# One index copy for two groups of gathers in the first two edge passes of a graph network

## The reference, cut to what matters

```python
# layer 0: messages along the edges, then a GRU cell
src_h = h[src] @ W_msg.T + b_msg
msg = src_h + edge_embed[clip(edge_type_9)]
messages = segment_sum(msg, dst, num_segments=12500)
x = x + gru_cell(messages, h)
...
# layer 1: graph convolution
msg = (deg_inv_sqrt[row] * deg_inv_sqrt[col])[:, None] * h[row]
agg = segment_sum(msg, col, num_segments=12500)
x = x + layernorm(agg @ W.T + b) * gamma + beta
```

## Time and profile before

| | us |
|---|---|
| median of 3 runs | 10787.66 |
| lowest and highest of them | 10783.5, 10787.84 |
| the profiled execution, its own time | 10766.11 |
| span of its trace | 10764.3 |
| first pass: first copy of indices to last | 127.5 to 2441.3 |
| second pass: first copy of indices to last | 2491.0 to 4811.0 |

### The profile page before, as it was taken

How to read it: one execution, slowest core, us unless ns; L and a number is a source line. 1 busy time by engine, 2 the same in 40 slices (tenths; PEclk the granted TensorE clock), 3 DMA queues, 4 the chain that set the end, 5 groups by cost and what they waited for, 6 DMA issues and landing times. The chain is left out here.

```text
span 10764.3 us, 142924 instructions
## 1 busy us (share of the span) xinstructions
PE 7296.1 (68%) x34582; PEld 5598.5 (52%) x34582; DVE 4890.2 (45%) x12591; ACT 1824.8 (17%) x4365; POOL 7100.4 (66%) x7075
## 2 busy tenths in 40 slices
PE   2655556555566666668888888888836666666666
PEld 1444445443333333336777777777624555555555
DVE  5444444445566666663222222222264555555556
ACT  1111111111111111112222222222221111111111
POOL 3666666665666666666888888888816555555553
PEclk6555555555555555556777777777755555555555
DMA  6122221222222222224444444444472222222221
GB/s 237 57 58 57 59 59 57 59 59 60 77 73 76 75 75 77 76 71 64 55 55 55 55 55 55 55 55 55 52 214 68 68 67 69 67 66 68 65 68 50
DMA packets 809415, 765.67 MB, mean 71 GB/s; under 512 B 128472, under 2 KB 701362, under 8 KB 809073
## 3 DMA queue, kind: packets, MB, share of 16 engines
q0 software_dynamic: 375872, 414.65, 21.5%
q1 hardware_dynamic: 340391, 271.94, 8.2%
q10 hardware_dynamic: 92938, 77.03, 2.3%
HBM read 544.72 MB, written 224.78 MB: 71 GB/s over the span
## 5 line engine op out<-in xcount | busy, mean ns | idle before, releaser
L1408 POOL DMA_INDIRECT scat<-msg_out,msg_idx x1564 | 2432.7, 1555 | 491.8 <-issue 421.7
L1997 POOL DMA_INDIRECT soft_rows<-proj,soft_slot x1564 | 1488.0, 951 | 1360.6 <-DVE soft_x L2184 690.2
L723 POOL DMA_INDIRECT L_rows<-H,L_slot x1568 | 1502.0, 958 | 691.3 <-issue 652.4
L988 POOL DMA_INDIRECT L_rows<-H,L_slot x1568 | 1498.2, 955 | 684.5 <-issue 618.0
L1501 PE MATMUL msg_ps_msg<-msg_hb,msg_lhs 128*128 128x128 f32 x6272 | 1600.3, 437 | 1.2 <-DVE msg_lhs L1474 1.2
L1501 PEld LDWEIGHTS msg_ps_msg<-msg_hb,msg_lhs 128*128 128x128 f32 x6272 | 1493.0, 328 | 191.8 <-issue 190.3
L1474 DVE SCALAR_TENSOR_TENSOR msg_lhs<-msg_dst_sp,msg_node,msg_ps_c 128x512 f32<-128x512 f32 x784 | 551.1, 745 | 2056.4 <-ACT msg_dst_sp L1429 2032.6
L859 PE MATMUL L_sum<-L_onehot,L_rows 128*128 128x64 f32 x3136 | 699.8, 394 | 782.9 <-issue 693.5
L859 PEld LDWEIGHTS L_sum<-L_onehot,L_rows 128*128 128x128 f32 x3136 | 648.7, 303 | 865.7 <-issue 851.8
L2126 PE MATMUL soft_ps_sum<-soft_onehot,soft_x 128*128 128x64 f32 x3136 | 753.1, 422 | 317.2 <-DVE sums_b L2243 226.1
L2126 PEld LDWEIGHTS soft_ps_sum<-soft_onehot,soft_x 128*128 128x128 f32 x3136 | 705.5, 328 | 383.9 <-issue 283.7
(11 more groups left out here) (365 smaller groups left out, 10487.9 us busy)
## 6 DMA issues: line engine op xcount, KB each, us to landing
L_rows<-H,L_slot POOLq DMA_INDIRECT x3136
msg_hb<-HB SPq DMA_DIRECT2D x392, 128.0 KB
soft_at_in<-in_edge_attr_dram SPq DMA_DIRECT2D x195, 256.0 KB
scat<-L_zeros SPq DMA_DIRECT2D x64, 408.0 KB
rel_parts<-scat SPq DMA_DIRECT2D x100, 256.0 KB, 5.0
HB<-L_prod ACTq DMA_DIRECT2D x49, 512.0 KB
scat<-msg_out,msg_idx POOLq DMA_INDIRECT x1564
soft_rows<-proj,soft_slot POOLq DMA_INDIRECT x1564
```

Of the source, the lines that this page charges most:

```text
L723: pool.indirect_dma_start(rows[:, k, j, :], None, t["H0"], bass.IndirectOffsetOnAxis(ap=slot[:, k, j:j + 1], axis=0)).then_inc(gathered[k] ...
L988: pool.indirect_dma_start(rows[:, k, j, :], None, t["H1"], bass.IndirectOffsetOnAxis(ap=slot[:, k, j:j + 1], axis=0)).then_inc(gathered[k] ...
L1408: pool.indirect_dma_start(t["scat"][j], bass.IndirectOffsetOnAxis(ap=idx[:, k, j:j + 1], axis=0), out[:, k, j, :], None, compute_op=ALU.ad ...
L1997: pool.indirect_dma_start(rows[:, s % SC, j, :], None, t["proj"], bass.IndirectOffsetOnAxis(ap=slot[:, s, j:j + 1], axis=0)).then_inc(gath ...
```

## The change

In `gather` of both passes, the copy of indices is made for two groups at once, at the even groups: it copies 8 columns of src_i into two neighbouring slots of the tile slot. It waits for a semaphore value that is one higher than the even group's own, and counts idx_ready up by 2. The eight gathers of the two groups follow one upon the other. The odd group has no copy and no wait of its own. The gathers themselves, their semaphores and all other engines' programs are as before.

```diff
@@ first pass, gather
-                pool.wait_ge(multiplied, r * GB + s + 1)
-                pool.tensor_copy(slot[:, k, :], t["src_i"][:, ds((i * GB + s) * J, J)]).then_inc(idx_ready, 1)
-                pool.wait_ge(idx_ready, r * GB + s + 1)
-                pool.nop(nofuse=True)
+                if s % 2 == 0:
+                    pool.wait_ge(multiplied, r * GB + s + 2)
+                    pool.tensor_copy(slot[:, k:k + 2, :].rearrange("p a j -> p (a j)"), t["src_i"][:, ds((i * GB + s) * J, 2 * J)]).then_inc(idx_ready, 2)
+                    pool.wait_ge(idx_ready, r * GB + s + 2)
+                    pool.nop(nofuse=True)
                 for j in range(J):
                     pool.indirect_dma_start(rows[:, k, j, :], None, t["H0"],
                                             bass.IndirectOffsetOnAxis(ap=slot[:, k, j:j + 1], axis=0)
```

## The result

The changed kernel is slower by 1.0%. On one chip it took 10897.76 us (10882.57 to 10901.4, four runs) and the kernel before 10787.75 us (10783.5 to 10801.17, four runs): a ratio of 1.010, 95% interval 1.0086 to 1.0114. The profiled execution took 10895.29 us, its span 10893.5 us. 110 us were lost where 228 us were to be won.

The account below looks back on a forecast made before the run. GpSimd's chain of copies and gathers was taken to bound both edge passes. Saving 267 us and adding 39 us of stops gave -228 us, from 10788 to 10560 us; range 10440 to 10700 us.

Parts of the forecast that it names:

- What the change removes: GpSimd, each pair: one copy and the way to the first gather go, an ordinary pause comes; 0.69 us less.
- cheap copy of eight: GpSimd's copy of 8 instead of 4 elements a partition: 0.01 us more a pair; dear case the whole 0.20 us again.
- The wait moves: GpSimd's copy for even group n needs group n-7 multiplied, not n-8: 28 more stops of 1.4 us, 39 us added.
- 8/7: Factor on the number of GpSimd's stops, for one slot fewer of the eight at the check.
- GpSimd's chain sets the pace: Both edge passes: GpSimd's chain without slack, 5.70 us a group, plus some 1.4 us of stop every eleventh to twelfth group.
- The equal pace of the two passes: Groups start 5.92 and 5.93 us apart despite different work on other engines; the reason for taking GpSimd's chain as bound.
- a stop at most pairs: Rival: the others live on breaks between groups, GpSimd stops at most pairs, slower, 11014 us if at all; chance 0.09.
- turning point: Number of stopped pairs from which the change turns slower: 241 of 392, at 1.5 us a stop.
- The 693.5 us put down to nothing: First pass: time ahead of TensorE's sums without a named cause; read as rows lying ready, other engines some groups behind.
- The transfers as the bound: Rival: the rows' transfers take the 5.70 us of a group, so no change, 10788 us; chance 0.02.
- Rarer stops: Rival: half as many checks, so GpSimd's 68 stops halve, 48 us more saved, 10473 us; chance 0.10.
- the other engines as a bound in themselves: Rival: they bound one pass or both, so savings return as stops; 10674 us (0.09) or 10788 us (0.04); chance 0.13.

Follow-up runs that it names:

- free-running: TensorE multiplies zeros without waiting for rows, GpSimd waits only for its own old gathers; one copy a group 11952.55 us, one for two groups 12924.49 us.
- own checks: Against the kernel before: one index copy for two groups, but each group waits for its own slot alone; 10921.32 us, ratio 0.9995.
- narrow rows: Against the kernel with zero tiles, no waits for rows and one copy for two groups: gathered rows of 16 bytes in place of 512; 12858.01 us.
- longer pause: Against the kernel with zero tiles, no waits for rows and one copy a group: a second small copy and its wait in each group; 10848.97 us.
- second copy in each group: Against the kernel before, everything computed: a second small copy and its wait in each group; ratio 1.0119.

## Why the prediction was wrong

*What the change removes* was right, 0.74 us a pair for 0.68, and the cheap copy of eight was right.

*"The wait moves"* is the step that failed. It priced the added stops at 39 us, 28 more of them at 1.4 us; they came to 404 us, 158 more and 2.2 us each. It let GpSimd's pace change (5.70 to 5.36 us a group) and kept the others' fixed at 7.15 us. But the others' pace hangs on GpSimd's: free-running, 10.9 us a group becomes 44.5 when GpSimd goes from 5.69 to 5.34 us. What was saved on GpSimd came back as stops for TensorE's late counts. The earlier check, to which the step gave its 8/7, costs nothing by itself; that the joint check adds the last per cent is suggested by the ratios 0.9995 with own checks and 1.010 with the joint one, taken on two occasions.

*"GpSimd's chain sets the pace"* was half right. It had no slack, but it was also the reason why the others lagged. (Nor did the sum come out: 5.70 us and the stops give 5.82 us a group, and 5.92 were measured; the pauses between gathers, 17 of 1.66 us in a pass, are 0.06 of the rest.) The equal pace of the two passes, 5.92 and 5.93 us, was taken as the sign of a bound on GpSimd alone. It may as well be the pace at which gathers leave the others just enough; with the chain at 5.33 us (own checks) the time stayed the same.

*The rival "a stop at most pairs"* names the mechanism, that the others live on the breaks, and nearly the count: 226 of 392 pairs. It was given 0.09, because breaks stood in each group of the earlier trace rows and the additions still came 7.15 us apart. That was the wrong reading: these breaks are why it was 7.15 us and not more. And its turning point, 241 pairs at 1.5 us, was too high as the stops are longer: (290 + 95) / 2.2 = 175 pairs. At its own 1.5 us the 226 stops would still have come out faster (10788 - 267 - 95 + 339 = 10765 us). The 693.5 us put down to nothing ahead of TensorE's sums were the sign. Rows did lie ready, but what the sums waited for can be named: 671 us of it, in 207 of the 254 waits, end within 0.3 us of the end of VectorE's addition two groups before, and VectorE waited for TensorE's late count (the "remote" of the earlier trace rows).

*The transfers as the bound* falls as far as bytes go: with the narrow rows the additions come as far apart (44.1 us for 44.5). *Rarer stops* and *the other engines as a bound in themselves* fall too: free of gathers they need 3.0 us a group in the first pass, and 4.3 us in the second once its gathers are over. By the rule of the Trainium skill that the prediction weighed ("DMA: Bandwidth & Descriptors", section "SWDGE vs HWDGE vs iDMA"), starting a DMA is usually small beside the DMA. By it the time would have stayed; here the starting is what costs, on GpSimd (5.70 us a group) and in the counts of TensorE, and in the free-running kernel the rows' size plays no part.

## What to carry to other kernels

Where one engine issues indirect DMAs back to back, the idle time of the others that is put down to nothing, or to a count that nothing seems to make, may be that engine's doing, so their pace must not be held fixed in an estimate that makes it issue faster. Take the dependency away (a still operand, no wait) and run both sides free: that shows in two runs what a saving is worth, and a pause that does nothing can be worth more than the work it replaces. Where a row names no cause of a wait, take from the program what is waited for, and set the end of that beside the end of the wait. A balance of a saving against stops needs the stop's number and its length from the new pace, not from the old.

## What was not expected of the hardware

GpSimd's indirect gathers, 0.94 us each with 0.30 us between, hold products of TensorE that depend on none of them, and make the counts by which TensorE reports its products late. Of the 3136 small products in the first pass 130 start after more than 0.5 us of idle time in the kernel before and 215 in the changed one; without gathers, and with the second copy in each group, none does. The other direction is prompt: TensorE's products follow the end of VectorE's addition by 0.24 us at 259.27, and by 0.14 us at 1067.35 of the free run. The effect is steep: additions 3.5 us apart at 6.01 us a group of gathers, 10.9 at 5.69, 44.5 at 5.34. TensorE's clock may have a part in it: from 163.7 us to 1518 us of the first pass the granted clock is 0.63 with the longer pause and 0.51 without it (at 1.2 GHz all the time it would be 0.50), so an engine that is held also runs slower; two levels of clock that lie a factor of two apart can't explain a factor of three. What in the chip is shared is open. Loading of instructions by DMA does not show as the cause: its two queues moved 12 packets in the first pass of the kernel before and 11 in that of the free run with one copy for two groups. The page "SBUF — State Buffer" of the Trainium skill (section "Who interferes with whom") knows only one contention between engines, that of VectorE and GpSimd for a shared pair of ports, and says that TensorE never waits there. These runs show TensorE's products, with no semaphore to wait for, 2.1 to 3.5 us apart while GpSimd issues; so either the rule does not cover issuing, or the hold is not at SBUF, and no run here tells which. Two things stand in the traces for whoever looks further. Single products come late only at some places of TensorE's loop of eight groups: in the kernel before, of the eight small products of the seventh group, 108 of 392 starts lie over 0.55 us behind the one before, and none of the eighth, first and second. And in the pass of scatters, with GpSimd issuing 1.55 us long DMAs 0.30 us apart, TensorE runs 16 products in a row undisturbed.
